# A DRAM scratch laid out in another order, so that stack transfers read and write 8 KB rows instead of 1 KB rows

## What is computed

```python
k, q, v = proj(W_key), proj(W_query), proj(W_value)      # (b, 16 heads, 512, 16), each * 256 ** -0.5
scores = einsum('bhqd,bhkd->bhqk', q, k) * 16 ** -0.5    # causal mask, softmax
out = einsum('bhqk,bhkd->bhqd', softmax(scores), v)      # then W_proj * 256 ** -0.5
x = layernorm(x + out)
scores_t = swapaxes(softmax(x @ router_w.T), 1, 2)
gate_vals, sel_idx = top_k(scores_t, 129)                # for each sequence and expert
y = gelu(tokens @ w1 + b1) @ w2 + b2                     # tokens = x at sel_idx
x = layernorm(x + zeros.at[sel_idx].add(y * gate_vals))
```

## Time and profile before

| | |
|---|---|
| median of 3 runs | 985.91 us (981.85 to 986.39) |
| time of the profiled execution | 987.11 us |
| its span, first to last instruction | 985.4 us |
| TensorE busy | 853.1 us (87% of the span) |
| mean granted clock of TensorE | 0.929 |
| attention's loads from `part_d` | 192 of 128 KB |
| stores to `part_d` | 96 of 128 KB |

### The profile page before, as it was taken

One profiled execution on the slowest core, in us unless ns is written; L12 is line 12 of the kernel. 1 busy time (PEld: TensorE's weight loads), 2 busy tenths in 40 slices (PEclk: granted clock), 3 DMA queues, 4 the chain that ended last, 5 costly groups with the idle time before them and its releaser, 6 DMA issues. The chain is left out here.

```text
span 985.4 us, 17316 instructions
## 1 busy us (share of the span) xinstructions
PE 853.1 (87%) x6044; PEld 647.9 (66%) x6044; DVE 655.1 (66%) x1957; ACT 524.4 (53%) x994; POOL 523.8 (53%) x621
## 2 busy tenths in 40 slices
PE   4568899999999999888669599998989999898990
PEld 3334455564646454434359589998989989898990
DVE  4457677888787778889938974646464644646454
ACT  3026666657666656555518245554555546455555
POOL 5336565556565563323545527657474655747443
PEclk9669999999999999988859799998999989999995
DMA  4987667777776758310142314344242342512248
GB/s 132 161 156 120 118 120 140 141 140 141 134 136 103 132 104 145 128 41 2 44 150 76 112 23 65 77 92 118 47 116 36 79 92 33 135 29 38 39 125 249
DMA packets 90166, 100.26 MB, mean 102 GB/s; under 512 B 9056, under 2 KB 83552, under 8 KB 89952
## 3 DMA queue, kind: packets, MB, share of 16 engines
q1 hardware_dynamic: 72288, 77.66, 37.8%
q0 software_dynamic: 12800, 16.92, 10.2%
q10 hardware_dynamic: 4992, 4.59, 1.4%
HBM read 65.12 MB, written 33.62 MB: 100 GB/s over the span
## 5 line engine op out<-in xcount | busy, mean ns | idle before, releaser
L497 DVE CUSTOM_DVE_ANT_0 n_ps<-n_ps,tri 128x512 f32<-128x512 f32 (+3 forms) x512 | 237.2, 520 | 73.6 <-PE n_ps L622 72.3
L1055 DVE TENSOR_TENSOR h_lo<-g,h_hi 128x384 fp32r<-128x384 f32 (+1 forms) x184 | 138.1, 759 | 129.2 <-ACT h_hi L991 120.8
L411 ACT ACTIVATE pt<-st_ps 128x512 f32<-128x512 f32 x320 | 181.8, 603 | 77.1 <-PE st_ps L607 70.0
L1131 PE MATMUL y_ps<-w_parts,h_hi 128*128 128x256 f32 (+1 forms) x1152 | 212.4, 279 | 0.0
L986 ACT ACTIVATE g<-h_ps,b 128x384 f32<-128x384 f32 (+1 forms) x192 | 104.2, 543 | 195.5 <-PE h_ps L1117 159.6
L1117 PE MATMUL h_ps<-tt_hi,w_parts 128*128 128x384 f32 (+1 forms) x768 | 179.2, 338 | 30.6 <-issue 20.0
L359 POOL TENSOR_SCALAR_AFFINE_SELECT pt<-pt 128x256 f32<-128x256 f32 (+1 forms) x320 | 111.3, 361 | 147.4 <-ACT pt L411 145.9
L1131 PEld LDWEIGHTS y_ps<-w_parts,h_hi 128*128 128x128 f32 (+1 forms) x1152 | 171.8, 177 | 3.3 <-ACT h_hi L991 0.2
L958 POOL DMA_INDIRECT acc<-y,tok_no x64 | 103.1, 1611 | 117.1 <-DVE y L1069 106.4
L1131 PE MATMUL y_ps<-w_parts,h_lo 128*128 128x256 f32 (+1 forms) x576 | 160.6, 279 | 0.0
L1117 PEld LDWEIGHTS h_ps<-tt_hi,w_parts 128*128 128x128 f32 x768 | 134.1, 200 | 32.9 <-issue 31.7
(11 more groups left out here) (149 smaller groups left out, 1152.4 us busy)
## 6 DMA issues: line engine op xcount, KB each, us to landing
w_parts<-part_d SPq DMA_DIRECT2D x192, 128.0 KB, 6.6
w_raw<-in_w SPq DMA_DIRECT2D x16, 1024.0 KB
part_d<-w_raw SPq DMA_DIRECT2D x96, 128.0 KB, 7.4
w_raw<-in_xt SPq DMA_DIRECT2D x8, 512.0 KB, 4.5
res<-in_x SPq DMA_DIRECT2D x8, 512.0 KB, 10.8
x<-res SPq DMA_DIRECT2D x8, 512.0 KB, 6.6
acc<-res SPq DMA_DIRECT2D x8, 512.0 KB, 8.2
fin<-acc SPq DMA_DIRECT2D x4, 512.0 KB, 4.1
```

What stands on the lines that cost most here:

```text
L411: nc.scalar.activation(pt[:, slot % PT_RING, n % UP, :], st_ps[at % ST_RING][:, :], ACT.Exp, scale=S_SCALE).then_inc(exp_done, 1)
L497: ins = nc.vector.tensor_tensor_reduce(out=src[:, h, :], in0=src[:, h, :], in1=mask, scale=-1.0, scalar=-BIG_NEG, op0=ALU.add, op1=ALU.min ...
L1055: nc.vector.tensor_tensor(h_lo[:, q % 2, n, 0:cols], g[:, at % G_RING, 0:cols], h_hi[:, q % 2, n, 0:cols].bitcast(F32), ALU.subtract).then ...
L1131: ins = nc.tensor.matmul(y_ps[at % Y_RING][0:rows, 0:C], x[:, q % 2, m, toks], w[e % 2][:, m, :], start=i == 0, stop=i == len(terms) - 1)
```

## The change

The scratch keeps its size. A (part, half) block of it was 128 rows of 512 bf16 in the order (head, row of the head); now it is in the order (row of the head, head). A load of a block is then 16 rows of 4096 bf16 (8 KB) on both sides. A store still reads 128 partitions of 1 KB; its DRAM side is now a pattern of 8 x 16 rows of 1 KB whose neighbours lie 8 KB apart.

```diff
-    part_d = nc.dram_tensor("part_d", [2, 2, 3, 2, P, T], BF16).ap()
+    part_d = nc.dram_tensor("part_d", [2, 2, 3, 2, D, HH, T], BF16).ap()
...
                 for part in range(3):
-                    sp.dma_start(part_d[which, b % 2, part, half_, :, :], parts[:, tile % 2, part, :]).then_inc(parts_out[tile % 2], 16)
+                    sp.dma_start(part_d[which, b % 2, part, half_, :, :, :].rearrange("d h n -> h d n"), parts[:, tile % 2, part, :]).then_inc(parts_out[tile % 2], 16)
...
                     for at, part in enumerate(blocks):
-                        src = part_d[which, b % 2, part, n, :, :].rearrange("(h d) n -> d h n", d=D)
+                        src = part_d[which, b % 2, part, n, :, :, :]
                         sp.dma_start(stack[at * D:(at + 1) * D, b % 2, HH * n:HH * (n + 1), :], src).then_inc(stack_in[n][b % 2], 16)
```

## The result

The changed kernel takes 992.9 us (median of 6 runs, 991.48 to 996.17); the kernel before takes 984.91 in the same 6 rounds. The ratio is 1.008, with a 95% interval of 1.006 to 1.010: slower by 0.8%. The profiled execution took 992.77 us, its span is 991.0 us.

A forecast was written before the change was run, and what follows sets the result against it. The start was taken to be bound by a chain of loads, stores and landings, the loop by TensorE. First stores +0.8, legs +6.0 and loads -0.8 gave +6.0 us on 985.9, so 992; range 978 to 1000.

The forecast's parts named there:

- The stores run on 8 engines: Scratch stores: DRAM side's outermost count of 8 halves the engines from 16; a leg's six drain in 4.5 us, not 2.2.
- The loads gain nothing by longer rows: Stack loads: 8 KB rows bring no gain from length; bounds 0 to -2.3 us in three legs, -0.8 taken.
- leg 1: First part of the start's chain: loads from 21.66 us, stores behind them, next loads at 37.31; +2.0 us forecast.
- The first stores, +0.8 us: Start, stores of tiles 0 and 1 gating the first loads: third store done 1.0 us later, some hidden, +0.8 taken.
- The legs, +2.0 us each: Start, three rounds of loads then six stores: slower drain adds 2.2 us each, 2.0 taken, +6.0 in all.
- Leg 2: Second part of the start's chain, 37.31 to 55.39 us, transfer of x ahead; +2.0 forecast, x using the free engines.
- Leg 3: Last part of the start's chain, from 55.39 us, ending when TensorE gets the nm transfers at 72.30; +2.0 us forecast.
- leg 3 step: End of the start: nm transfers taken to wait for the slower stores behind the loads; +2.0 us.
- Nothing in the loop: Loop: stores slower by 0.4 us each, but DMA has room and no scratch transfer is waited for; cost 0.
- The sum: Whole run: 0.8 + 6.0 - 0.8 = +6.0 us, all before 72.3 us; median 992.

The follow-up runs named there:

- e2: Kernel before with one unused scratch row after each head: stores 8 x 16 rows as in the change, loads still 1 KB rows; 992.42 us, ratio 1.0075.
- e1: Kernel before with q and k weight columns permuted on the host: loads of 8 KB rows, each store one block of 128 rows; 986.89 us, ratio 1.0014.
- e3: Kernel before with the twelve loads reordered, both stacks' blocks alternating so neighbours write the same partitions or 0 and 32; 991.97 us, ratio 1.0065.
- e6: e1 with parts adjacent in the scratch and stack blocks reordered: seven loads of 48, 32 or 16 partitions for twelve; 977.0 us, ratio 0.9903 against kernel before.
- e4: e1 with 64 unused bytes behind each scratch row, so loads are of 1 KB rows; 989.89 us, ratio 1.0051.

## Why the prediction was right

The time was forecast at 992 and measured at 992.9, by the mechanism that it named. That the two lie within 1 us is in part luck: the forecast had +6.0 us, all of it in the start; the medians say +8.0, and the profiles find 3.4 to 4.3 of it in the start. Two terms were off, in opposite directions.

- **The stores run on 8 engines.** Right, and it is the whole loss: e2 has it with the old loads, e1 lacks it with the new ones. By the Trainium skill, "DMA: Bandwidth & Descriptors", section "Why a DMA increments its semaphore by 16 and not by 1", 128 against 8 gives 8. The trace agrees with 67,894 packets and a drain of 160 to 170 GB/s (177 and 189 in e2); 175 was forecast.
- **The loads gain nothing by longer rows.** Right in the argument. The 0.8 us that I still gave them is neither shown nor excluded: from leg 1 to the first score matmul e1 takes 49.5 us where the kernel before takes 50.6 and 50.0, but the changed kernel takes 52.0 and 52.7 where e2 takes 51.8. What holds them are their destination partitions: 113 to 115 GB/s where neighbours share a set, 124 to 134 where they don't, 180 and 184 with more partitions a load. By the Trainium skill, "SBUF — State Buffer", section "Door 1: The DMA port swizzle", partitions 0 and 32 lie on one port and 0 and 16 on two; e3 and e6 agree with it.
- **The first stores, +0.8 us.** Mis-sized: +2.05 and +1.6 in the two pairs of profiles. I reckoned with three stores. But at 0.69 us each (128 KB at 190 GB/s, an estimate) those of tile 0 are not done when those of tile 1 come, and the queue now holds six in a row.
- **The legs, +2.0 us each.** Leg 1: +1.9 and +1.1. Leg 2: -0.3 and +1.2. Leg 3, from its first issue to the score matmul: 16.91 and 16.62 before, 16.66 and 17.11 after, so about +0.1. So leg 2 gave less than the 2.0 in both pairs, and the leg 3 step failed. I had let the nm transfers wait for the stores behind the loads. In the changed kernel their 48 packets start between 73.9 and 74.8 us while the stores still drain, 14.9 to 15.8 us after the leg's first issue, as before (70.4 to 71.2 us, 15.0 to 15.8 after it, in the first profile). In e3, whose stores are as before and whose loads are slower, they begin 16.3 us after it. So their time goes with the loads, not with all of the stores behind these. What fills the 2 us between the end of the last load (71.9) and their first packet (73.9) is not shown.
- **Nothing in the loop.** Nearly right: no transfer of the scratch is waited for after the start, but every period with such stores is 0.2 us longer, some 1.2 us in six (an estimate). No wait in the profile of a period has grown by more than 0.3 us, and its cause stays open. The window of 48 us that the prediction calls a period (96 to 144 us) is a piece of one; a period is 51.9 us before. And the loop holds the stores of six sequences, not seven.
- **The sum.** In the profiles the start costs 3.4 and 4.3 us (forecast: 6.0), and at the last store of x1 it is 5.4 and 5.0. The medians say 8. The part between them is not explained. Stretches at a granted clock of 0.97, each worth 1.5 us, (53.4 us for a period instead of 51.9) fall elsewhere in each profile, so that single profiles can differ by 1.5 us for this reason alone.

## What to carry to other kernels

Longer rows can help a transfer only if the length of its rows holds it. Here the 16 destination partitions did, as rows of 1 KB into 128 partitions at 336 GB/s had already suggested, and the way to a gain was more partitions in each load: seven loads for twelve gave 1%. When a layout is turned, look at both sides of every transfer that touches it. An outermost count of 8 on the DRAM side halved the engines of the stores, at the same bytes and the same rows; turning the producer's rows instead (a permutation of weight columns, e1) cost nothing that the runs can tell: 1.0014, 0.9998 to 1.0030.

## What the runs showed of the hardware

- A store of 128 KB with an outermost count of 8 takes 0.575 us to issue on SP (changed kernel, e2), one with 128 takes 0.432 (kernel before). A load of 16 x 8 rows of 1 KB takes 0.60 us to issue where the 8 rows of a partition lie 1088 bytes apart (e4), and 0.431 where they lie 16 KB apart (before). These are medians over the run.
- The order of otherwise equal loads in one queue changes their rate: 113 to 115 GB/s with neighbours at the same partitions or at 0 and 32 (e3), 124 to 134 with neighbours at 0 and 16 (before).
